# A three-stage graph, attention and expert kernel: three kept adjacency groups per row in place of two, a ring of five in place of eight, and the rotary halves exchanged by transfers

## The reference

```
h   = layernorm(x)
A   = adj + I;  d = sum(A, axis=1) ** -0.5
x1  = x + relu((d[:,None] * A * d[None,:]) @ (h @ W.T))     # graph
z   = layernorm(x1);  h2 = rmsnorm(z) * ln1
q, k, v = h2 @ wq.T, h2 @ wk.T, h2 @ wv.T                   # 4 heads of 32, 2 key/value heads
q = q * cos + rotate_half(q) * sin;  k likewise             # rotate_half: (-upper half, lower half) of each head
```

## Time and profile before

| what | value |
|---|---|
| median of three runs | 3580.86 us |
| profiled execution, and its span | 3581.53 us, 3579.8 us |
| TensorE busy over the span | 3099.7 us (87%) |
| VectorE busy over the span | 2571.3 us (72%) |
| adjacency loads into the ring (1 MB each) | 302 |
| adjacency loads into kept slots (1 MB each) | 45 |
| phase one, phase two (to 1333 us) | 869 us, 464 us |

### The profile page before, as it was taken

How to read it: one execution, slowest core, us unless ns; L and a number is a source line. 1 busy time by engine, 2 the same in 40 slices (tenths; PEclk the granted TensorE clock), 3 DMA queues, 4 the chain that set the end, 5 groups by cost and what they waited for, 6 DMA issues and landing times. The chain is left out here.

```text
span 3579.8 us, 56821 instructions
## 1 busy us (share of the span) xinstructions
PE 3099.7 (87%) x22369; PEld 1361.4 (38%) x22369; DVE 2571.3 (72%) x2752; ACT 1424.0 (40%) x2843; POOL 1684.5 (47%) x1082
## 2 busy tenths in 40 slices
PE   2678889899899969999999999999999999829990
PEld 1334434344444433433333333333333333315650
DVE  8888886764554537779778877778877888227774
ACT  0000000000000004656666666666766666726660
POOL 0000000000212214666887689777789778734664
PEclk9778999999999978999999999999999999969995
DMA  9898875777768834522220000000000000012226
GB/s 379 337 385 360 360 311 241 311 300 260 269 259 328 327 131 159 209 88 85 100 70 10 10 24 18 7 13 7 11 18 18 1 12 9 13 66 59 72 66 238
DMA packets 170430, 531.94 MB, mean 149 GB/s; under 512 B 20721, under 2 KB 66938, under 8 KB 125254
## 3 DMA queue, kind: packets, MB, share of 16 engines
q1 hardware_dynamic: 124328, 473.74, 34.3%
q10 hardware_dynamic: 33024, 31.47, 2.6%
q0 software_dynamic: 12816, 23.11, 2.0%
HBM read 434.70 MB, written 92.15 MB: 147 GB/s over the span
## 5 line engine op out<-in xcount | busy, mean ns | idle before, releaser
L1231 DVE TENSOR_REDUCE unit_max<-ps_max 128x2 f32<-128x1024 f32 (+2 forms) x1088 | 1226.0, 1171 | 309.3 <-PE ps_max L1460 265.0
L1007 POOL TENSOR_TENSOR chunk_sum<-chunk_sum,probs 128x1024 f32<-128x1024 f32 x480 | 1132.1, 2359 | 309.0 <-ACT probs L1101 299.1
L1101 ACT ACTIVATE probs<-ps_ring 128x512 f32<-128x512 f32 x2112 | 1089.8, 596 | 437.3 <-PE ps_ring L1479 404.2
L566 PE MATMUL ps_gather<-ring,keep_attended 128*128 128x512 f32 x1688 | 791.6, 626 | 140.4 <-DMA ring<-in_adj 121.7
L1479 PE MATMUL ps_ring<-q_stack,keep_shared 97*128 97x512 f16 x2112 | 674.6, 385 | 28.3 <-ACT probs L1101 22.8
L1494 PE MATMUL ps_acc<-probs,keep_shared 128*32 128x256 f32 (+1 forms) x8448 | 565.3, 386 | 0.0
L566 PEld LDWEIGHTS ps_gather<-ring,keep_attended 128*128 128x128 f32 x1688 | 333.3, 202 | 542.7 <-issue 542.7
L367 DVE TENSOR_TENSOR work<-work,ring 128x2048 f32<-128x2048 f32 x195 | 446.6, 2290 | 36.0 <-DMA ring<-in_adj 32.4
L342 POOL DMA_DIRECT2D scratch_lower<-lower x13 | 7.3, 559 | 807.7 <-ACT lower L484 807.7
L1460 PE MATMUL ps_max<-k_heads,q_heads 32*128 32x512 f16 (+3 forms) x2176 | 275.6, 378 | 68.9 <-DVE unit_max L1231 47.4
L1503 PE MATMUL ps_acc<-probs,keep_ones_heads 128*32 128x256 f32 (+1 forms) x4224 | 327.3, 379 | 0.0
(11 more groups left out here) (244 smaller groups left out, 2669.2 us busy)
## 6 DMA issues: line engine op xcount, KB each, us to landing
ring<-in_adj SPq DMA_DIRECT2D x302, 1024.0 KB, 14.1
keep_shared<-in_adj SPq DMA_DIRECT2D x45, 1024.0 KB, 11.1
scratch_slots<-empty_rows SPq DMA_DIRECT2D x16, 2080.0 KB, 14.1
scratch_parts<-empty_part SPq DMA_DIRECT2D x8, 2048.0 KB, 13.3
moe_parts<-scratch_parts SPq DMA_DIRECT2D x64, 256.0 KB, 4.4
moe_x_rows<-scratch_slots SPq DMA_DIRECT2D x39, 260.0 KB, 2.7
x_in<-in_x SPq DMA_DIRECT2D x16, 256.0 KB, 13.4
x_in<-in_x ACTq DMA_DIRECT2D x16, 256.0 KB, 8.0
```

Of the source, the lines that this page charges most:

```text
L566: last = nc.tensor.matmul(bank[:], support[:, s * SUB + c, :], tile_of[g, is_again][:, c * BT:(c + 1) * BT], start=(first and c == 0), sto ...
L1007: steps.then(nc.gpsimd.tensor_tensor(totals, totals, weights, ALU.add))
L1101: nc.scalar.activation(probs[:, q % SLOTS, i, kv, :, lo:], halves(bank)[:, :, lo:], ACT.Exp, scale=SCALE).then_inc(ring_read, 1)
L1231: nc.vector.tensor_reduce(unit_max[:, half % 2, heads, s % 2, unit], ps_max[:, base:base + HEADS, at:at + width], AX_X, ALU.max).then_inc( ...
```

## The change

KEPT_SPAN goes from 2 to 3: the groups (t, t+1) to (t, t+3) and the diagonal stay, so 78 groups are read again and the closing groups of a row are four from row 4's on. That takes ten slots: the six in `shared` and four in a new tile `own_kept`. The ring shrinks from eight buffers to five, and TensorE's accumulating banks grow from four to five. The permuted weights and their two projections go. In their place VectorE multiplies q and k by a sine table with the sign swapped (`crossed`), eight transfers of 16 partitions x 4 KB issued by ScalarE exchange the halves of each head into `swapped`, and VectorE adds them in a new step `split`, which has its own place in `due` one group after the former `rotate`, and so behind `normalize` of the next strip. The waits for the stores of the former strip move from `rotate` into `split`, and ScalarE issues the stores of strip n-1 (`store_split`) behind the exchange of strip n and the loads of cos and sin.

```diff
-    R = 8
-    KEPT_SPAN = 2
+    R = 5
+    KEPT_SPAN = 3
...
+    due += [(begins[n] + 6, 3, n) for n in range(NB)]
...
-        KEPT_SLOTS = 6
+        KEPT_SLOTS = 10
+        SHARED_SLOTS = 6
         ring = sb("ring", [P, R, SUB * BT])
+        own_kept = sb("own_kept", [P, KEPT_SLOTS - SHARED_SLOTS, SUB * BT])
...
-        rope_a, rope_b = work[:, 2], work[:, 3]
+        crossed = work[:, 2:4]
+        swapped = sb("swapped", [P, 2, BT])
...
-        ps_q, ps_q_half, ps_k, ps_k_half = ps_support, ps_gather[2], ps_gather[3], ps_degrees
+        ps_q, ps_k = ps_support, ps_gather[3]
+        ps_again = [ps_gather[(NB - BANKS + n) % BANKS] for n in range(2)]
...
-            for w, d in ((wT, "wT"), (wq, "wq"), (wq_half, "wq_half"), (wk, "wk"), (wk_half, "wk_half"),
-                         (wv, "wv"), (ln1, "ln1")):
+            for w, d in ((wT, "wT"), (wq, "wq"), (wk, "wk"), (wv, "wv"), (ln1, "ln1")):
...
             def rotate(n):
                 if n:
+                    dve.wait_ge(split_ready, 2 * n)
+                dve.wait_ge(tables_loaded, n * 32 + 32)
+                dve.wait_ge(qk_ready, n + 1)
+                for m, plain in enumerate((ps_q, ps_k)):
+                    nc.vector.tensor_tensor(crossed[:, m], plain[:], sin, ALU.mult).then_inc(crossed_ready, 1)
+                    nc.vector.tensor_tensor(rotated[m][:], plain[:], cos, ALU.mult).then_inc(crossed_ready, 1)
+
+            def split(n):
+                if n:
                     dve.wait_ge(split_stored, n * 48)
                     if n <= STACKED_BY_POOL:
                         dve.wait_ge(keys_stacked, n * 96)
                     else:
                         dve.wait_ge(last_stacked, (n - STACKED_BY_POOL) * 96)
-                dve.wait_ge(tables_loaded, n * 32 + 32)
-                dve.wait_ge(qk_ready, n + 1)
-                for m, (plain, half, hi) in enumerate(((ps_q, ps_q_half, q_hi), (ps_k, ps_k_half, k_hi))):
-                    nc.vector.tensor_tensor(rope_a, plain[:], cos, ALU.mult)
-                    steps.then(nc.vector.tensor_tensor(rope_b, half[:], sin, ALU.mult))
-                    steps.then(nc.vector.tensor_tensor(rotated[m][:], rope_a, rope_b, ALU.add))
+                dve.wait_ge(crossed_ready, 4 * n + 4)
+                dve.wait_ge(swapped_in, SWAPS * (n + 1))
+                for m, hi in enumerate((q_hi, k_hi)):
+                    steps.then(nc.vector.tensor_tensor(rotated[m][:], rotated[m][:], swapped[:, m], ALU.add))
                     steps.then(nc.vector.tensor_copy(hi[:], rotated[m][:]))
                 dve.sem_inc(high_ready, 1)
...
+            def swap_halves(n):
+                act.wait_ge(crossed_ready, 4 * n + 4)
+                for row in range(0, NH * HD, HD):
+                    for to, src in ((row, row + HD // 2), (row + HD // 2, row)):
+                        act.dma_start(swapped[to:to + HD // 2], crossed[src:src + HD // 2]).then_inc(swapped_in, 16)
+
+            def store_split(n):
+                act.wait_ge(split_ready, 2 * n + 2)
+                cols = slice(finished[n] * BT, (finished[n] + 1) * BT)
+                for name, tile in (("q_hi", q_hi), ("q_lo", q_lo), ("k_hi", k_hi)):
+                    act.dma_start(dram[name][:, cols], tile[:]).then_inc(split_stored, 16)
...
-                act.wait_ge(high_ready, n + 1)
+                swap_halves(n)
                 if n + 1 < NB:
                     load_tables(n + 1)
-                act.wait_ge(split_ready, 2 * n + 2)
-                cols = slice(t * BT, (t + 1) * BT)
-                act.dma_start(dram["q_hi"][:, cols], q_hi[:]).then_inc(split_stored, 16)
-                act.dma_start(dram["q_lo"][:, cols], q_lo[:]).then_inc(split_stored, 16)
-                act.dma_start(dram["k_hi"][:, cols], k_hi[:]).then_inc(split_stored, 16)
+                if n:
+                    store_split(n - 1)
+            store_split(NB - 1)
...
-                    pe.wait_ge(high_ready, n)
+                    pe.wait_ge(crossed_ready, 4 * n)
...
-                for out, w in ((ps_q, wq), (ps_q_half, wq_half), (ps_k, wk), (ps_k_half, wk_half)):
+                for out, w in ((ps_q, wq), (ps_k, wk)):
```

More of the change, by code:

```diff
@@ L159, in graph_stage @@
         x1, z = by_subtile(work[:, 0]), by_subtile(work[:, 1])
-        rope_a, rope_b = work[:, 2], work[:, 3]
+        crossed = work[:, 2:4]
         cos, sin, hT = work[:, 4], work[:, 5], work[:, 6]
-        rotated = [sb(f"rotated{n}", [P, BT]) for n in range(2)]
-        reduced = [sb(f"reduced{n}", [P, BT]) for n in range(2)]
+        swapped = sb("swapped", [P, 2, BT])
+        reduced = [swapped[:, n] for n in range(2)]
         inv_sqrt_degree = sb("inv_sqrt_degree", [P, NB * SUB])
@@ L178, in graph_stage @@
         wT = sb("wT", [C, C])
[L179 to L180 removed]
+        wq, wk = sb("wq", [C, C]), sb("wk", [C, C])
         wv = sb("wv", [C, NKV * HD])
@@ L184, in graph_stage @@
         complete = {t: sb(f"complete{t}", [P, BT]) for t in whole}
-        q_hi, q_lo = sb("q_hi", [P, BT], F16), sb("q_lo", [P, BT], F16)
-        k_hi, k_lo = sb("k_hi", [P, BT], F16), sb("k_lo", [P, BT], F16)
+        rotated = [own_kept[:, 0, n * BT:(n + 1) * BT] for n in range(2)]
+        q_hi, q_lo, k_hi, k_lo = (own_kept[:, 0, 2 * BT + n * BT // 2:2 * BT + (n + 1) * BT // 2].bitcast(F16)
+                                  for n in range(4))
         BANKS = KEPT_SPAN + 2
@@ L191, in graph_stage @@
         ps_support = ps("ps_support", [P, BT])
-        ps_degrees = ps("ps_degrees", [P, BT])
-        ps_degree = ps_degrees[:, 0:SUB]
-        ps_q, ps_q_half, ps_k, ps_k_half = ps_support, ps_gather[2], ps_gather[3], ps_degrees
-        ps_v = ps("ps_v", [P, SUB, NKV * HD])
+        ps_v_and_degrees = ps("ps_v_and_degrees", [P, BT])
+        ps_v = ps_v_and_degrees[:, 0:SUB * NKV * HD].rearrange("p (s c) -> p s c", s=SUB)
+        ps_degree = ps_v_and_degrees[:, SUB * NKV * HD:SUB * NKV * HD + SUB]
+        ps_q, ps_k = ps_support, ps_gather[3]
+        ps_again = [ps_gather[(NB - BANKS + n) % BANKS] for n in range(2)]
         ring_loaded = [sem(f"ring_loaded{s}") for s in range(R)]
@@ L232, in graph_stage @@
         z_ready = sem("z_ready")
+        crossed_ready = sem("crossed_ready")
+        swapped_in = sem("swapped_in")
         high_ready = sem("high_ready")
@@ L253, in graph_stage @@
                 kept_until[slot] = s if s > t else t
-                tile, semaphore = shared[:, slot], kept_loaded[slot]
+                tile = shared[:, slot] if slot < SHARED_SLOTS else own_kept[:, slot - SHARED_SLOTS]
+                semaphore = kept_loaded[slot]
             else:
@@ L266, in graph_stage @@
         STACKED_BY_POOL = NB - 2
+        SWAPS = 2 * NH * 16
         def stack_keys(queue, n, stacked):
@@ L409, in gather_strip @@
                     dve.wait_ge(support_ready, NB)
-                nc.vector.tensor_tensor(gathered[turn % 2][:], ps_gather[turn % 2][:], lower[turn % 2][:], ALU.add
+                nc.vector.tensor_tensor(gathered[turn % 2][:], ps_again[turn % 2][:], lower[turn % 2][:], ALU.add
                                         ).then_inc(strip_gathered, 1)
@@ L462, in _ @@
             for _, kind, n in sorted(due):
-                (gather_strip, rotate, normalize)[kind](n)
+                (gather_strip, rotate, normalize, split)[kind](n)
         @block.scalar
         def _(act):
-            act.wait_ge(weights_loaded, 16 * 7)
+            act.wait_ge(weights_loaded, 16 * 5)
             def root_degrees(t):
@@ L547, in turn @@
                 last.then_inc(signal, 1)
-            pe.wait_ge(weights_loaded, 16 * 7)
+            pe.wait_ge(weights_loaded, 16 * 5)
             pe.wait_ge(constants_ready, 9)
@@ L2011, in rotary_tables @@
     emb = np.concatenate([freqs, freqs], axis=-1)
-    sign = np.where(np.arange(HD) < HD // 2, -1.0, 1.0).astype(np.float32)
+    sign = np.where(np.arange(HD) < HD // 2, 1.0, -1.0).astype(np.float32)
     cos, sin = np.cos(emb), np.sin(emb) * sign
@@ L2026, in laid_out @@
     adj = a["adj"].reshape(NB, BT, NB, SUB, P).transpose(0, 2, 4, 3, 1).reshape(NB, NB, P, SUB * BT)
-    half = np.concatenate([np.arange(HD // 2, HD), np.arange(HD // 2)])
     q_rows = np.arange(NH * HD).reshape(NH, HD)
@@ L2035, in laid_out @@
         "x": a["x"], "adj": adj, "wT": a["gnn_W"].T,
-        "wq": wq[q_rows.ravel()].T, "wq_half": wq[q_rows[:, half].ravel()].T,
-        "wk": wk[k_rows.ravel()].T, "wk_half": wk[k_rows[:, half].ravel()].T,
+        "wq": wq[q_rows.ravel()].T, "wk": wk[k_rows.ravel()].T,
         "wv": a["ffn_wv"].T, "wo": a["ffn_wo"].T, "ln1": a["ffn_ln1_w"][:, None], "ln2": a["ffn_ln2_w"][:, None],
```

4 lines of the change are left out of this document (2 added, 2 removed).

## The result

The changed kernel takes 3658.18 us (median of four runs, 3649.95 to 3662.34); the kernel before 3579.32 (median of four). The ratio is 1.0216 [1.0196, 1.0236]. It is slower, as forecast, but by 79 us in place of 11, and outside the range. The profiled execution took 3658.9 us; its span is 3657.1. Of the four runs of `order`, a version further down, one (3565.78 us at a granted clock of 0.901, the others at 0.944 to 0.946) was in a slower state of the chip and is left out of that version's figures.

A forecast was written before the change was run, and what follows sets the result against it. It took loads to bound rows 1 to 3 of phase one, TensorE the rest, with a hole per row, and phase two. 83.4 - 41.6 - 27.4 - 9 + 6 = +11.4 gave 3593 us, range 3567 to 3632.

The forecast's parts named there:

- phase one, +83.4: Stretch to the degrees of row 15: 41.6 for added groups, 19.7 for holes, 22.1 for the shorter ring.
- The gates: Rows 1 to 3, loads waiting for an early group's multiplication: ring of five puts nine more loads ahead, +22.1 us.
- the holes: TensorE's idle time per row behind queued kept loads: grows to about 9.1 us in rows 5 to 12, +19.7.
- row 4's: Hole of row 4: the older backlog may hide the added load; 0 to 2.5 us, taken as 0.
- groups moved: Thirteen second reads go; 12 groups move from phase two to phase one, 41.6 us each way, worth nothing alone.
- projections: Phase two: two of four projections go in each of 16 strips, 27.4 us less.
- Waits of phase two: TensorE's idle time in phase two: one new hole, one old wait left, about 9 us less than before.
- Rotation: Phase two: exchanges issued in 3.7 us, landing in 4 to 7, hidden; 3 us of slack per strip.
- rival C: Transfers bind phase two, as each strip moves 7.9 MB with the exchange: 3607 us, or 3612; chance 0.08.
- B: The exchange lands late and `split` holds the next rotate up to 5.8 us: 3633 us; chance 0.17.
- The end, +6: Last strip, nothing to hide behind: exchanges, stores and landing +7.0, former strip's projection +1, last projection saves 2 more.

The follow-up runs named there:

- order: Kernel before the change, with each row's kept loads queued behind all its ring loads: 3504.70 us (median of three), 0.9777.
- kept: Changed kernel with three groups kept and ring of five, but the four projections, rotate and stores of before: 3621.79 us, 1.0110.
- ring5: Kernel before the change with a ring of five buffers in place of eight, nothing else: 3598.45 us, 1.0043.
- noexch: Changed kernel with the eight exchanges neither made nor awaited, so the halves are stale: 3589.54 us, 1.0032.
- thin: Changed kernel with each exchange carrying only the first eighth of its bytes, so results are wrong: 3616.33 us, 1.0096.
- traffic: `kept` plus transfers of the exchange's shape between SBUF places, issued by GpSimd and read by nobody: 3642.38 us, 1.0168.
- poolswap: Changed kernel with GpSimd issuing the eight exchanges in place of ScalarE: 3632.60 us, 1.0143.
- early: Changed kernel with ScalarE issuing the former strip's stores behind hT of the next strip, ahead of the exchanges: 3633.43 us, 1.0141.
- poolearly: Changed kernel with both GpSimd issuing the exchanges and the former strip's stores issued early: 3629.36 us, 1.0137.
- rot: Kernel before the change with only the exchange by transfers; ring of eight and two kept groups stay: 3649.55 us, 1.0199.

## Why the prediction was wrong

**Right: phase one, +83.4.** It measured +79.0, and +81.6 in `kept`. The gates were reproduced alone by `ring5`, the holes by the rows above. By parts, the changed kernel's third gate comes 19.3 us later (22.1 forecast), the holes of rows 5 to 12 grew by 20.6 (19.7), and row 4's, taken as unchanged, by 2.3 (9.35 to 11.69).

**Right: groups moved, and projections.** Phase two lost 44.4 us in `kept`: TensorE's busy time fell by 42.9 (41.6 forecast for the groups), and 26.5 more went in `noexch` (27.4 for the projections). But *Waits of phase two*, -9, failed: TensorE's idle time was 47.9 us before, 46.4 in `kept` and 45.2 in `noexch`. That `noexch`, with 393.3 us, meets the forecast's 392 is thus partly luck: 392 holds those 9 us, and at the end 5.6 us for an exchange that `noexch` doesn't make. What `noexch` shows is that VectorE's new order costs nothing by itself.

**Wrong: Rotation, "I take the shorter kind with a load or two ahead, 4 to 7 us: hidden."** The exchange, put at nothing in phase two, cost 64.3 us there (457.6 against the 393.3 of `noexch`). Three things failed in that step. The landing itself was sized well (median 5.5 us), but it was not the cost. First, the issues, counted at 0.46, took 0.61 each (median), and "ahead of the statistics of normalize, which ask for it at about 8" was left without a term: the roots stand behind the exchanges, the tables and three stores. With the small transfers themselves that is the 23.0 us between `noexch` and `thin`. Second, the 0.5 MB a strip had no term in the sum (only rival C priced it, at the rate of the loads); it holds the DMA engines 2.6 us a strip, 42 in all, and seven eighths of the bytes cost 41.3 us of time. That the two figures are so near is no proof that one is the other, since `traffic` lost only 18.5 by the same bytes. Third, in the changed kernel the cost shows at transfers whose delay had no term: the issue of x1's store blocks, and the former strip's stores come late. The slack of 3 us a strip is spent: TensorE waits for `normed` 12 times, 63.9 us in all.

**The rivals.** B has the nearest time (3633) and the right place, `split` and the strip's chain, but the wrong mechanism: in the changed kernel's profile no wait ends with the exchange's landing (the longest took 10.8 us). That wait appears only when the issues are put right, in `poolswap`, `early` and `poolearly` (13.7, 33.9 and 44.2 us). C is nearer to the cause, with too small a price. The DMA engines' busy share in 40 equal slices of phase two (tenths; 9 is 90% or more), first before, then changed:

```profile
DMA  9172389994048999489992499976999789440401
```

```profile
DMA  9159379999399889569997979898799989673341
```

They are full in 17 slices before and in 19 after. So "a phase where DMA doesn't bind (share 0.73)", in *Groups moved*, took a mean over full and empty stretches for the state of each. In the full slices they move 393 GB/s before, 372 in `noexch` and 334 in the changed kernel: the exchange's bytes, at 5.0 us a MB, take engine time from the loads and stores beside them. The Trainium skill, page "DMA: Bandwidth & Descriptors", section "Where 436 GB/s comes from", gives about 358 GB/s for the HBM side. The runs disagree: in `noexch` the engines moved 414 GB/s over 21 us.

```profile
1072.60:1093.60 21.00, 20.79 (x61) 10.27 (x62) 6.84 (x16) 1.47 (x4) 2.27 (x2) 1.00 1.03 414
```

The same page, section "Issuing engines are not separate DMA queues", says that transfers issued by several engines share the same DMA engines, so that another issuer saves only issue time. The runs agree: with GpSimd as issuer and the stores early the roots were in time, yet phase two stayed 29 us above `noexch` (the median of whole runs 40).

**The end, +6.** From the last second-read group to attention 35.5 us became 48.3: +12.8. From the last strip's projections on, where the exchange lies, 22.4 us became 27.7, about as forecast (7 less 2). Ahead of them 13.1 became 20.6, where +1 was forecast: one more strip's projections fall there (`noexch`: 16.4), and the root of the last `normalize` is 2.62 us late behind the former strip's exchange.

What stays open: why a MB between two SBUF places takes 5.0 us of the engines. The transfers have 16 partitions each, and whether larger pieces would be cheaper was not tried. Nor is it split further how much of the 41.3 us is the blocked issue and how much late stores; `traffic` shows only that 18.5 come without any wait for the bytes. In `rot` phase two is 62 us longer although the projections' 27 are saved, so the exchange costs about 89 there, against 64 in the changed kernel; that was not taken apart. (The ring of eight, which alone lengthened phase two by 17 us, is one difference.)

## What to carry to other kernels

Price an added transfer three times: its issue, by what stands behind it on the issuing queue; its bytes, by the engine time per MB of that kind of transfer, not of another; and its landing. A transfer whose landing is hidden can still be the most expensive thing in the change. And when an engine idles for a load, look first at what stands ahead of that load in its queue: two gated loads a row ahead of ungated ones cost this kernel 79 us, more than either half of the change could bring.

## What the runs showed of the hardware

- An exchange between SBUF partitions here, 64 KB in 16 partitions: 0.61 us (median) to issue from ScalarE, 0.48 from GpSimd, 5.5 us to land under load, and 5.0 us of the sixteen DMA engines' time a MB, against 2.8 for the 1 MB loads beside it.
- The issue of a plain store can hold its engine's sequencer: for x1's 0.33 us with no exchange traffic, up to 7.49 with it (for z's up to 2.83 without and 2.79 with it), and a root that only stands behind it is late by that much.
- A mean DMA share hides full stretches: at 0.69 over phase two of the kernel before, the engines were 90% busy or more in 17 of 40 slices.
- A deeper ring is not always better: eight buffers in place of five gained 31 us in phase one and lost 17 in phase two, where VectorE waited 38.5 us for the strips' small stores with eight and not at all with five. The longest landing of k_hi's store was 18.3 us with eight and 13.3 with five, but the median 4.9 and 8.8; that it was the loads issued ahead of need that held the stores up is not shown.
